# Token tiles split into halves in SBUF and turned by DMA transposes in place of TensorE transposes

## What is computed

```
x = x + attn_a(_layernorm(x))                          # causal, 16 heads of 16, q = k = v
x = x + ffn(_layernorm(x), Wr, W1, b1, W2, b2)         # mixture: two of eight experts per batch
x = x + attn_b(_layernorm(x), Wq, bq, Wk, ... Wo, bo)  # distance attention, one head of 256
x = x + ffn(_layernorm(x), Wr, W1, b1, W2, b2)         # the mixture again, same weights
```

## Time and profile before

| | |
|---|---|
| time, median of 3 runs | 1665.28 us (1665.22 to 1665.33) |
| the profiled execution's own time | 1663.65 us |
| its span in the trace | 1661.9 us |
| granted TensorE clock | 0.999 |
| PE busy | 1615.9 us, 97% |
| DVE busy | 1072.7 us, 65% |
| ACT busy | 988.1 us, 59% |
| POOL busy | 305.7 us, 18% |

### The profile page before, as it was taken

How to read it: one execution, slowest core, us unless ns; L and a number is a source line. 1 busy time by engine, 2 the same in 40 slices (tenths; PEclk the granted TensorE clock), 3 DMA queues, 4 the chain that set the end, 5 groups by cost and what they waited for, 6 DMA issues and landing times.

```text
span 1661.9 us, 27980 instructions
## 1 busy us (share of the span) xinstructions
PE 1615.9 (97%) x10531; PEld 755.2 (45%) x10531; DVE 1072.7 (65%) x2182; ACT 988.1 (59%) x1261; POOL 305.7 (18%) x402
## 2 busy tenths in 40 slices
PE   6999999999999999999999999999999899999998
PEld 2222222222233444444445666666666544444444
DVE  7533454354336865885557688868998886576554
ACT  6999999999997333533335555555445433353332
POOL 2012112112120000000005345544444200000000
PEclk9999999999999999999999999999999999999999
DMA  4012334100130003000000000000000200300000
GB/s 138 17 47 95 91 122 145 26 14 14 27 103 1 1 1 102 1 1 1 1 0 1 2 1 1 1 1 1 1 1 27 77 1 1 127 13 14 13 14 26
DMA packets 44338, 52.73 MB, mean 32 GB/s; under 512 B 3671, under 2 KB 39086, under 8 KB 44206
## 3 DMA queue, kind: packets, MB, share of 16 engines
q1 hardware_dynamic: 44206, 50.96, 9.8%
HBM read 38.88 MB, written 4.19 MB: 26 GB/s over the span
## 4 chain that ended last, share of the span: by engine, by line
PE 67%; ACT 16%; issue 10%; DVE 5%; POOL 1%; DMA 0%; ACTq 0%; DVEq 0%; SPq 0%; POOLq 0%
ACT a_probs L779 15%; PE f_h L1038 7%; PE f_ypsum L1039 7%; PE f_ypsum L1040 7%; PE f_ypsum L1038 7%; PE f_h L1039 7%; PE f_h L1040 7%; PE a_out L539 3%; PE d_outs L1038 3%; PE d_outs L1040 3%; PE d_outs L1039 3%; PE d_banks L1038 2%; PE d_banks L1039 2%; PE d_banks L1040 2%; PE a_scores L913 2%
## 5 line engine op out<-in xcount | busy, mean ns | idle before, releaser
L779 ACT ACTIVATE a_probs<-a_scores 128x1024 f32<-128x1024 f32 x544 | 499.9, 1210 | 6.6 <-PE a_scores L913 6.4
L1398 ACT ACTIVATE f_gelu<-f_h,f_bcol,s_more 128x512 f32<-128x512 f32 x256 | 199.1, 778 | 405.3 <-PE f_h L1040 393.8
L539 PE MATMUL a_out<-a_probs,a_values 128*32 128x512 f32 (+3 forms) x2560 | 293.3, 539 | 6.9 <-ACT a_probs L779 5.5
L1461 DVE TENSOR_SCALAR f_hh<-f_gelu,f_gates_scaled 128x512 f16<-128x512 f32 x256 | 125.0, 488 | 199.9 <-ACT f_gelu L1398 198.6
L1907 ACT ACTIVATE d_score<-d_dist,d_nksq,s_more 128x512 f32<-128x512 f32 x128 | 104.1, 814 | 191.1 <-DVE d_dist L2052 189.3
L1463 DVE SCALAR_TENSOR_TENSOR f_hl<-f_gelu,f_gates_scaled,f_hh 128x512 f16<-128x512 f32 x256 | 192.3, 751 | 9.1
L913 PE MATMUL a_scores<-a_moving,a_fixed 64*128 64x512 f16 (+3 forms) x1280 | 183.6, 353 | 9.7 <-ACT a_probs L779 3.7
L1944 POOL TENSOR_TENSOR distance_raw<-distance_raw,d_p 128x512 f32<-128x512 f32 x112 | 146.6, 1309 | 177.4 <-ACT d_p L1882 177.3
L793 POOL TENSOR_SCALAR_AFFINE_SELECT a_probs<-a_probs 128x256 f32<-128x256 f32 (+1 forms) x224 | 98.0, 453 | 419.5 <-ACT a_probs L779 417.7
L1038 PE MATMUL f_h<-c_xhi,f_w 128*128 128x512 f16 x384 | 145.6, 379 | 1.7 <-DVE f_w L1114 1.7
L1039 PE MATMUL f_h<-c_xlo,f_w 128*128 128x512 f16 x384 | 145.5, 379 | 0.0
(11 more groups left out here) (268 smaller groups left out, 2475.6 us busy)
## 6 DMA issues: line engine op xcount, KB each, us to landing
f_raw<-in_L_ffn_W SPq DMA_DIRECT2D x16, 1024.0 KB, 7.6
f_raw<-in_L_ffn_W SPq DMA_DIRECT2D x24, 512.0 KB, 8.1
a_fixed<-a_moving SPq DMA_DIRECT2D x60, 96.0 KB, 2.3
x<-in_L_attn_a_x SPq DMA_DIRECT2D x7, 512.0 KB, 6.3
out<-x SPq DMA_DIRECT2D x7, 512.0 KB, 2.9
f_raw<-in_L_ffn_W SPq DMA_DIRECT2D x12, 256.0 KB, 3.4
a_fixed<-a_moving SPq DMA_DIRECT2D x60, 32.0 KB, 2.0
f_early_raw<-in_L_ffn_W SPq DMA_DIRECT2D x4, 256.0 KB, 3.3
```

The costliest lines, as they stand in the source:

```text
L539: mm = pe.matmul(spare[32 * j:32 * j + 32, i % 2, skip:skip + w], values[:, G % 2, kt + tile, j, :], probs[:, u % UR, j % 2, col:col + w], ...
L779: act.activation(probs[:, u % UR], scores[:, 2 * (u % SR):2 * (u % SR) + 2, :], ACT.Exp, scale=HD ** -0.5)\
L1398: act.activation(gel[:, n % HR, :], hps[:, n % 2, :], ACT.Gelu, bias=mix.bcol[:, q, FT * e + j:FT * e + j + 1], scale=pr.scales.hidden)\
L1461: dve.tensor_scalar(hh[:, n % HR, :], gel[:, n % HR, :], gate, None, ALU.mult).then_inc(s_hh, 1)
```

## The change

The order of splitting and turning is swapped. A normalised pair is split while its tokens still lie on the partitions, in SBUF, into `c_tokens_hi` and `c_tokens_lo` (float16, two pairs each). Each half is then turned by DMA transposes that SP issues, eight of 128x128 for a pair, straight into the rings `c_xhi` and `c_xlo`, which grow to eight pairs. PE has no transposes of tokens any more; where it uses a pair it waits for the DMAs' semaphore (`turned`).

```diff
-    RING = 4
+    RING, PARTS = 8, 2 * 2 * KD
...
     def norm(self, dve, u):
         pr = self.pr
         if u >= 2:
-            dve.wait_ge(self.s_turn, u - 1)
+            dve.wait_ge(self.s_lo, u - 1)
...
+    def high(self, act, u):
+        act.wait_ge(self.s_xn, 2 * u + 2)
+        if u >= 2:
+            self.turned(act, u - 2)
+        act.activation(self.tokens_hi[:, self.place(u), :], self.xn[:, self.place(u), :], ACT.Copy, scale=self.scale(u))\
+           .then_inc(self.s_hi, 1)
...
+    def low(self, dve, u):
+        dve.wait_ge(self.s_hi, u + 1)
+        if u >= 2:
+            self.turned(dve, u - 2)
+        dve.scalar_tensor_tensor(out=self.tokens_lo[:, self.place(u), :], in0=self.xn[:, self.place(u), :], scalar=self.scale(u),
+                                 in1=self.tokens_hi[:, self.place(u), :], op0=ALU.mult, op1=ALU.subtract).then_inc(self.s_lo, 1)
+
+    def turn(self, sp, u):
+        sp.wait_ge(self.s_lo, u + 1)
         for i in range(2):
+            at = self.at(u).start + i * P
             for k in range(KD):
-                mm = pe.transpose(out[:, k, i * P:(i + 1) * P], self.xn[:, (2 * u + i) % self.RING, k * P:(k + 1) * P], self.pr.ident[:])
-        mm.then_inc(self.s_turn, 1)
...
+                for to, of in ((self.hi, self.tokens_hi), (self.lo, self.tokens_lo)):
+                    sp.dma_start(to[:, k, at:at + P], of[:, 2 * (u % 2) + i, k * P:(k + 1) * P], transpose=True)\
+                      .then_inc(self.s_col[u % 2], 16)
+
+    def turned(self, engine, u):
+        engine.wait_ge(self.s_col[u % 2], 16 * self.PARTS * (u // 2 + 1))
```

In the mixtures the pairs move to earlier steps, and the last chunk of the first mixture makes six pairs (16 to 21) in place of two:

```diff
-                for f, i in {7: 0, 10: 1}.items():
+                for i, f in enumerate((1, 3, 5, 7, 9, 11) if last_batch and c == CHUNKS - 1 else (1, 7)):
                     if f <= a <= f + 2:
-                        work.append((("norm", "turn", "low")[a - f], base + (TILES // 2) * q + 2 * (c + 1) + i))
+                        work.append((("norm", "high", "low")[a - f], base + (TILES // 2) * q + 2 * (c + 1) + i))
```

SP's program of a mixture turns a chunk's pairs first, and loads the second batch's experts behind the turns of chunk 2; the stores of the result follow between chunks:

```diff
-            chosen = mix.chosen(sp, 1, routing)
-            mix.load_biases(sp, 1, chosen)
-            mix.load_weights(sp, 1, chosen, range(len(mix.PIECES)))
+            for chunk in range(NB * CHUNKS):
+                if not (last_layer and chunk == LAST):
+                    turn(chunk + 1)
+                if chunk == CHUNKS // 2:
+                    chosen = mix.chosen(sp, 1, routing)
+                    mix.load_biases(sp, 1, chosen)
+                    mix.load_weights(sp, 1, chosen, range(len(mix.PIECES)))
+                if last_layer and chunk >= 1:
+                    store((chunk - 1) * TPC, TPC)
```

In the distance attention `AT` keeps `norm` for pairs 6 to 17 and has `high` and `low` in place of `turn`, one to three steps earlier; two of its lines:

```diff
-              44: [("norm", 8)],
-              45: [("norm", 9)],
-              47: [("turn", 8)],
+              44: [("norm", 8)],
+              45: [("norm", 9), ("high", 8)],
+              46: [("low", 8), ("high", 9)],
+              47: [("low", 9)],
```

More of the change, by code:

```diff
@@ L571, in _ @@
             mix.load_weights(sp, 0, chosen, range(len(mix.PIECES)))
+            for u in range(2):
+                cols.turn(sp, u)
         @block.vector
@@ L986, in __init__ @@
         self.pr = pr
-        self.xn = sb("c_xn", [P, self.RING, D], F32)
+        self.xn = sb("c_xn", [P, 4, D], F32)
+        self.tokens_hi = sb("c_tokens_hi", [P, 4, D], F16)
+        self.tokens_lo = sb("c_tokens_lo", [P, 4, D], F16)
         self.hi = sb("c_xhi", [P, KD, self.RING * 2 * P], F16)
         self.lo = sb("c_xlo", [P, KD, self.RING * 2 * P], F16)
-        self.s_xn, self.s_turn, self.s_hi, self.s_lo = pr.sems("cols", "xn", "turn", "xhi", "xlo")
+        self.s_xn, self.s_hi, self.s_lo = pr.sems("cols", "xn", "xhi", "xlo")
+        self.s_col = pr.sems("cols", *(f"turned{i}" for i in range(2)))
     def scale(self, u):
@@ L1269, in _, with turn, store @@
         def _(sp):
+            def turn(chunk):
+                if chunk > CHUNKS:
+                    sp.wait_ge(s_h, CS * (chunk - CHUNKS))
+                for i in range(6 if chunk > LAST else 2):
+                    if chunk > LAST and i in (2, 4):
+                        sp.wait_ge(s_h, CS * (chunk - CHUNKS + i // 2))
+                    cols.turn(sp, base + 2 * chunk + i)
+            def store(tile, tiles):
+                sp.wait_ge(s_added, (tile + tiles) // 2)
+                b, t = divmod(tile, TILES)
+                sp.dma_start(pr.out_d[b, t * P:(t + tiles) * P, :].rearrange("(t p) d -> p t d", p=P),
+                             x[:, tile:tile + tiles, :]).then_inc(pr.s_out, 16)
             all_read(sp)
@@ L1374, in do @@
             def do(kind, what):
-                if kind == "turn":
-                    cols.high(act, what, side[:])
+                if kind == "high":
+                    cols.high(act, what)
                 elif kind == "tanh":
@@ L1415, in do @@
                 elif kind == "low":
-                    cols.low(dve, what, side[:])
+                    cols.low(dve, what)
                 elif kind == "stats":
@@ L1668, in distance_attention @@
               105: [("norm", 16)],
-              106: [("norm", 17)],
-              107: [("turn", 16)],
-              109: [("turn", 17)],
+              106: [("norm", 17), ("high", 16)],
+              107: [("low", 16), ("high", 17)],
+              108: [("low", 17)],
               117: [("tanh",)],
@@ L1732, in _ @@
         def _(sp):
+            free_ahead(sp)
+            for p in range(6, TILES + 2):
+                if p >= cols.RING:
+                    sp.wait_ge(s_v, p - cols.RING + 1)
+                    g = (p - cols.RING) // 2
+                    sp.wait_ge(s_p, KD * (max(task["q", g], task["k", g]) + 1))
+                cols.turn(sp, BASE + p)
             chosen = mix.chosen(sp, 0, routing)
@@ L1745, in free @@
                 reads.clear()
-            def turn(p):
-                bank = turn_bank("turn", p)
-                if p != 2:
-                    free(turn_read)
-                    turn_read.append((cols.s_lo, BASE + p + 1))
-                cols.turn(pe, BASE + p, bank)
             def values(p):
-                bank = turn_bank("values", p)
+                bank = values_bank(p)
                 if p >= 1:
@@ L1889, in weights_high @@
                 mix.part_high(act, 0, i)
-            do = {"turn": high, "values": values_high, "project": project_high, "tanh": tanh, "weights": weights_high}
+            do = {"high": high, "values": values_high, "project": project_high, "tanh": tanh, "weights": weights_high}
             act.activation(rden[0:1, 0, 0:1], pr.ones[0:1, 0:1], ACT.Exp).then_inc(s_table, 1)
@@ L1896, in _ @@
             project_high(1, 1)
-            high(2)
-            high(3)
             values_high(0)
@@ L1956, in _ @@
                         add_squares(what[0])
-                    if kind == "norm" and what[0] < BASE:
+                    if kind in ("add", "norm") and what[0] < BASE:
                         add_bias(what[0])
```

119 lines of the change are left out of this document (45 added, 74 removed).

## The result

The changed kernel takes 1697.32 us (median; 1694.06 to 1698.83 in four executions), the kernel before 1665.25 us in the same session (1663.81 to 1665.33). The ratio is 1.0192, 95% interval 1.0174 to 1.021: slower by 32 us, where 18 us faster was forecast. The profiled execution took 1698.83 us, its span is 1697.0 us, 35.1 more than that of before. That is more than the 32 us between the medians, since this execution is the longest of its four and the one profiled before (1663.65 us) is shorter than its median.

The account below looks back on a forecast made before the run. TensorE was taken to bound the kernel in the mixtures (99.6% and 97.7% busy), ScalarE the head attention. 1663.65 - 21.2 gain + 2.4 + 0.2 waits = 1645.05, plus 1.6 to the median: 1647; likeliest range 1642 to 1660, all cases to 1690.

Parts of the forecast that it names:

- the new queue: SyncE issues 8 DMA transposes a pair, 384 in all, in order; 0.8 us each taken, landing 2.3 us after issue.
- T: Interval between DMA transposes on SyncE's queue, unknown from the trace; taken as 0.8 us, ends 0.60 and 1.86.
- the rival with 0.34: Slow queue: `high` waits for pair u-2 and waits cost more than the transposes did; 1679 at T = 1.3; chance 0.34.
- my range for all: All cases together: 1642 up to 1690, the top being 1687 at T = 1.4 plus 3 us for slower landing.
- 15T - 13.9: Start of the first mixture: wait for the sixteenth transpose's landing, wanted at 518.92; none under T = 0.93.
- 31T - 22.4: First mixture's last chunk, six pairs: wait of `high` for landings; 2.4 us at T = 0.8, none under 0.72.
- 31T - 28.7: Distance attention, steps 45 to 55: wait of `high` for the fourth pair's landing; 0.2 us forecast for T = 0.8.
- the range of the likeliest: Faster case, T under 1.08, chance 0.58: 1644 at T = 0.60, 1657 at T = 1.0, range 1642 to 1660.
- The choice of experts: Second batch's loads stand behind a chunk's transposes; done at 646.3, wanted at 648.72; no wait under T = 1.1.
- its start: Start of the distance attention: earlier normalisation lets GpSimd's sum of squares start sooner; 1.6 plus 0.5, 2.1 us gain.
- pairs 4 to 7: Distance attention: with pairs 12 to 15, where TensorE's steps are full, transposes counted in full, 8 x 0.44 = 3.5 us.
- half of 2.9: Crowded start of the distance attention: of 2.9 us without TensorE in 879 to 937, half counted as gain, 1.5.

Follow-up runs that it names:

- wide kernel: The changed kernel with four DMA transposes a pair, each of 128 tokens by 256 features, in place of eight; 1657.31 us, ratio 0.9955.
- filled wide kernel: The wide kernel plus 12 and 6 unread products on TensorE ahead of its waits for squared lengths in distance attention steps 7 and 63; 1651.48 us, ratio 0.9923.
- steps 6 and 9: The filled wide kernel with mixture chunk pairs at steps 6 and 9, not 1 and 7, and chosen experts' biases loaded ahead of that chunk's transposes; 1649.81 us.
- the doubling: The kernel before, with TensorE's transposes of distance pairs 4 to 15 made twice (8 in place of 4); 1667.18 us, ratio 1.0019.
- the kernel with the mixtures' chunks alone: The changed kernel with DMA transposes only for the 28 pairs standing two in a mixture chunk, the others turned on TensorE; 1655.94 us, ratio 0.9945.

## Why the prediction was wrong, by its own steps

**The step that failed** is the new queue: "I take 0.8, near the median, a third above it because a transpose is one instruction more complex than a copy". T is 1.306. The copy's row was the right row for a copy of these tiles (0.644 us) and the wrong one for a transpose of them. My bounds, 0.60 and 1.86, held it; the value taken lay at the wrong end, and the rival with 0.34 had the mechanism. It is not the only step: my range for all ended at 1690, worked with T = 1.4, and 1697 lies above it although T is less. What is missing beyond T are places and terms that I left out or put at nothing, listed below. The Trainium skill's table ("VectorE: DVE Perf Modes", The three transpose paths, 1309 ns by DMA) agrees with the interval here; the sentence of the Trainium skill in "Advanced Engine Details and Errata", X-Bar Transpose (TRN2), that such DMAs are as fast as regular ones does not, for tiles of 32 KB: 1.275 against 0.644 us.

**The formulas, with T right.** At 1.306: start of the mixture 15T - 13.9 = 5.7 us, measured 5.76. Last chunk 31T - 22.4 = 18.1, measured 17.3 + 2.3 = 19.6, where the 2.3 us is what the wide kernel gains on the same way with no wait; the 1.5 us over it are about the last step's half clock (4.3 in place of 2.6 us). Distance steps 44 to 67: 31T - 28.7 = 11.8. Measured are 13.3, less the 1.5 that the filled wide kernel loses there without a wait for the queue: 11.8, of which 1.7 are the low clock in step 64, so 10.1 for the waits; that the two 11.8 agree is in part luck. The first of these waits was not `high`'s but TensorE's own, for the last transpose of pair 9 in step 53, which I had not listed:

```profile
1087.67 0.58 PE L1045 MATMUL d_outs<-c_xhi,wk_hi 128*128 128x512 f16 x1 [4.58 <-DMA c_xlo<-c_tokens_lo]
```

That they all are queue waits is shown by the runs with 4, 6 and 8 instructions a pair. Redone, the working gives 1656 at T = 1.0 (it says 1657) and 1662 at T = 1.08, so the range of the likeliest, to 1660, did not reach its own condition.

**What the rival's 1679 still lacked** against 1697, worked on the span: 35.6 - 21.2 = 14.4 us foreseen at T = 1.306, 35.1 measured, 20.7 missing.
- Pairs 6 and 7, 8.3 us: I left this place out. At step 8 TensorE needs the sixteenth landing of a queue that could begin at 922.9; 922.9 + 15T + 2.3 = 944.8. Steps 0 to 11 are 6.4 us longer, in the filled wide kernel 1.9 shorter. Of the 8.3, 4.75 us are the wait itself; two stretches of half clock, from 935.3 and 945.5, are part of the rest, and how much was not tried apart.
- The moved normalisation, 2.2 us: I costed the earlier steps in the mixtures at nothing, beside VectorE's slack. But in step 3 of the first chunk TensorE waits 0.68 us for an expert's weights that VectorE makes behind it, and in step 20 of both mixtures, the second chunk's step 4, for the last chunk's result. At steps 6 and 9 these losses are gone, which shows it. The choice of experts adds 0.2 us in step 47.
- Gains in the distance attention that were not there, 5.9 us: 0.7 at its start (1.4 measured for 2.1), 1.4 at pairs 4 to 7 and the "half of 2.9", 3.8 in steps 44 to 67 (a loss of 1.5 for a gain of 2.3). What TensorE saves there it waits for: for VectorE in step 53, for GpSimd in steps 7, 55 and 63 of the wide kernel. For pairs 4 to 7 only the doubling shows that there was slack.
- The clock: 1.6 us from the stretch at 23.9 us, 1.0 in step 0 behind the wait, and about 1.5 in the last chunk.

These make 20.7 us.

**What was right.** A pair costs a mixture 0.44 us (0.437 measured in all 28 of the changed kernel). ScalarE's half from SBUF took 0.619 us, less than the 0.71 taken, and was hidden. Bytes played no part. In the last chunk the place of the waits, and `high` ahead of the GELU as their carrier, were as described. The choice of experts cost 0.2 us (step 47), where the working gives 1.6 at T = 1.306; in the kernel with the mixtures' chunks alone the same step cost 1.2, so the small figure is no proof of room.

## What to carry to other kernels

Before work is moved to a queue, count its instructions and find the issue time of that very kind of DMA; where the trace has none, the decision belongs at the break-even value (1.12 us by my working) and not at the nearest row. Even that value was too kind: six instructions a pair, which load the queue as T = 0.96 would, already gave the time of the kernel before. Fewer and wider DMAs can turn such a change round: four instructions in place of eight took it from 32 us slower to 7 us faster. A saving on TensorE counts only where no other engine arrives at the same time, and moved helper work needs a look at what its engine owes in the new step.

## What the hardware showed

- A DMA transpose from SBUF to SBUF costs SyncE's queue 1.23 to 1.25 us, for 128x128 and for 128x256 of 16 bits alike; a plain copy of the same 128x128 tile costs 0.60.
- Of the changed kernel's 384 transposes 20 held the queue for over 1.5 us (2.5 at most), and 37 landed more than 3 us after issue; nothing in these runs says why.
- TensorE's clock fell to the lower level after idle times of 1.3 us (step 63 of the wide kernel, before 1103.86) and more, for 3.4 or 6.8 us, but not after every one: it stayed at 1.00 after the 1.9 us before 1051.54. Where the next wait was for the queue, taking three slow stretches away won 0.9 us of 5.0; where TensorE was the bound, two gave 1.7 and 2.5 us. Products that nobody reads, put into the waits, took five of six such stretches away.
